# Attention scores of a causal kernel on one core: query and key parts as two float32r parts, two heads of a pair in the two row halves of the array

## The reference, cut to what matters

```
q, k = rotated (and in the first layer normalised) parts of x @ w_qkv
attn = einsum('bhqd,bhkd->bhqk', q, k) * scale        # D = 8 channels a head
attn = where(causal, attn, -inf); attn = softmax(attn)
out  = einsum('bhqk,bhkd->bhqd', attn, v)
```

```
scores = einsum('bhtd,bhsd->bhts', q, k) * mask        # decay in q and k
denom  = clip(abs(scores).sum(-1), 1, 50000)
ret    = einsum('bhts,bhsv->bthv', scores / denom, v)
```

## Time and profile before

| what | value |
|---|---|
| median of 3 runs | 2440.61 us (2437.79 to 2441.31) |
| the profiled execution, first to last instruction (span) | 2438.4 us |
| PE, DVE, ACT, POOL busy | 81%, 70%, 56%, 17% of the span |
| attention stages (first maximum to last output) | about 68 to 549, 1106 to 1588 and 1836 to 2320 us |
| stage of the retention heads | about 677 to 889 us |
| mean granted TensorE clock | 0.908 of full speed |

### The profile page before, as it was taken

How to read it: one execution, slowest core, us unless ns; L and a number is a source line. 1 busy time by engine, 2 the same in 40 slices (tenths; PEclk the granted TensorE clock), 3 DMA queues, 4 the chain that set the end, 5 groups by cost and what they waited for, 6 DMA issues and landing times. The chain is left out here.

```text
span 2438.4 us, 38777 instructions
## 1 busy us (share of the span) xinstructions
PE 1983.5 (81%) x13002; PEld 869.3 (36%) x13002; DVE 1703.7 (70%) x4395; ACT 1355.0 (56%) x1947; POOL 419.0 (17%) x670
## 2 busy tenths in 40 slices
PE   5689999994879974777799999957555899999939
PEld 3122333223534442553223333237331223332228
DVE  6688788847567767567788888632695887888433
ACT  4246666676379965334356666732543466666812
POOL 4000021020055521310001110133000010210133
PEclk9799999996989985988899999978867999999969
DMA  7600120001111100016101010014027001100024
GB/s 199 162 1 15 27 41 1 1 1 62 52 46 48 47 16 1 1 31 188 24 1 41 9 33 1 1 45 174 23 55 188 1 3 39 41 1 1 2 93 166
DMA packets 63781, 114.82 MB, mean 47 GB/s; under 512 B 12588, under 2 KB 45486, under 8 KB 62836
## 3 DMA queue, kind: packets, MB, share of 16 engines
q1 hardware_dynamic: 55668, 98.72, 14.9%
q0 software_dynamic: 5088, 11.24, 1.6%
q10 hardware_dynamic: 2860, 2.77, 0.3%
HBM read 64.78 MB, written 31.56 MB: 40 GB/s over the span
## 5 line engine op out<-in xcount | busy, mean ns | idle before, releaser
L1087 ACT ACTIVATE probs<-score 128x1024 f32<-128x1024 f32 x960 | 825.7, 897 | 542.2 <-PE score L1151 539.2
L1209 DVE TENSOR_REDUCE max_part<-stat 128x1 f32<-128x512 f32 x1152 | 721.9, 683 | 113.7 <-PE stat L1101 112.2
L1164 PE MATMUL pv<-probs,v_ones 128*9 128x512 f32 (+3 forms) x3840 | 443.7, 534 | 0.7 <-ACT out_turned L1078 0.5
L1206 DVE CUSTOM_DVE_ANT_0 masked_scores<-stat,mask_row 128x128 f32<-128x128 f32 (+3 forms) x768 | 343.2, 487 | 125.7 <-PE stat L1101 124.1
L1056 POOL TENSOR_SCALAR_AFFINE_SELECT probs<-probs 128x256 f32<-128x256 f32 x384 | 154.7, 408 | 1272.5 <-ACT probs L1087 1269.1
L1101 PE MATMUL stat<-first_group_k,first_group_q 128*128 128x512 bf16 (+2 forms) x960 | 301.1, 368 | 68.2 <-DVE max_part L1209 35.7
L1101 PE MATMUL stat<-group_k,group_q 128*128 128x512 bf16 (+2 forms) x960 | 288.5, 349 | 15.1 <-DVE max_part L1209 9.1
L1151 PE MATMUL score<-first_group_q,first_group_k 128*128 128x512 bf16 x960 | 262.8, 357 | 30.1 <-DMA first_group_q<-row_max_turned 29.0
L1151 PE MATMUL score<-group_q,group_k 128*128 128x512 bf16 x960 | 254.3, 350 | 5.8 <-DMA group_q<-row_max_turned 3.5
L1101 PEld LDWEIGHTS stat<-first_group_k,first_group_q 128*128 128x128 bf16 x960 | 93.9, 99 | 250.3 <-DVE max_part L1209 123.6
L1859 ACT ACTIVATE abs_act_ps<-abs_act_ps 128x1024 f32<-128x1024 f32 (+3 forms) x176 | 167.6, 952 | 27.8 <-PE abs_act_ps L1812 27.8
(11 more groups left out here) (369 smaller groups left out, 2318.3 us busy)
## 6 DMA issues: line engine op xcount, KB each, us to landing
tile_wv<-expert_wv SPq DMA_DIRECT2D x38, 512.0 KB
q_parts<-early_parts_t SPq DMA_DIRECT2D x20, 384.0 KB, 3.3
group_k<-k_parts SPq DMA_DIRECT2D x18, 384.0 KB
group_q<-q_parts SPq DMA_DIRECT2D x18, 384.0 KB
q_parts<-parts_t SPq DMA_DIRECT2D x17, 384.0 KB, 4.6
head_q<-q_parts SPq DMA_DIRECT2D x48, 96.0 KB
head_k<-k_parts SPq DMA_DIRECT2D x48, 96.0 KB
first_group_k<-k_parts SPq DMA_DIRECT2D x9, 384.0 KB
```

The lines of the kernel that those rows point to most:

```text
L1087: nc.scalar.activation(probs[:, n % PSLOTS, :, 0:width], sc[hp][:, :, 0:width], ACT.Exp, scale=scale).then_inc(expd.sem, 1)
L1164: last = nc.tensor.matmul(acc[32 * h:32 * h + D + 1, f:BANK], v9[:, kt, g * HG + h, :], probs[:, (2 * t + h // 2) % PSLOTS, h % 2, 0:BANK ...
L1206: nc.vector.tensor_tensor_reduce(masked[:, at % 2, 0:width], ring[n % RBANKS][:, 0:width], w["mask_row"][:, BANK - width:BANK], 1.0, NEG, ...
L1209: nc.vector.reduce_max(into, ring[n % RBANKS][:], AX.X).then_inc(stat_used.sem, 1)
```

## The change

Queries and keys are cut into two parts instead of three, each held as float32 and rounded to what the engine takes as float32r (`rounded` is a bitcast to that type). 2 x 2 x 8 = 32 rows carry a head. Rows are laid out in two halves of 64: head 0 and head 2 of a group in partitions 0 to 63 (32 product rows, 2 shift rows, constants), head 1 and head 3 in 64 to 127, and each score or maximum matmul names its half with `tile_position`. Row tensors have half as many columns (`PAIRS` = 2 instead of 4 heads) of twice the width. A group's rows come in four transfers of 16 partitions for keys and four for queries. The matmul that subtracts a part is float32r too. The retention heads keep one matmul over 128 rows, of which 96 are now zero. The constants of the padding come through an HBM tensor that the load stage fills.

```diff
-PARTS = 3
+PARTS = 2
 KROWS = PARTS * PARTS * D
+HROWS = 64
+PAIRS = HG // 2
...
+def rounded(ap):
+    return ap.bitcast(F32R)
...
+def head_rows(h):
+    return slice(HROWS * (h % 2), HROWS * (h % 2) + HROWS)
...
-    rows = k_dram.rearrange("(g h d) a t -> g (d a) h t", h=HG, d=D)
-    for a in parts:
-        eng.dma_start(tile[a * PARTS * D:(a + 1) * PARTS * D, :, cols], rows[g][:, :, cols]).then_inc(sig.sem, 16)
+    rows = k_dram.rearrange("(g p i d) a t -> g i (d a) p t", p=PAIRS, i=2, d=D)
+    for i in range(2):
+        for a in range(PARTS):
+            at = HROWS * i + a * PARTS * D
+            eng.dma_start(tile[at:at + PARTS * D, :, cols], rows[g, i][:, :, cols]).then_inc(sig.sem, 16)
...
                 for n in range(NQ):
                     turn(n)
-                    if n > 0:
-                        take_out(n - 1, 1)
                     if n + 2 < NQ:
                         project(n + 2)
                     take_out(n, 0)
-                take_out(NQ - 1, 1)
...
-        uq, uk = ([first_rows[n], k.sb(f"group_{what}", [P, HG, T], BF16, ctx)] for n, what in enumerate("qk"))
+        uq, uk = ([first_rows[n], k.sb(f"group_{what}", [P, PAIRS, T], F32, ctx)] for n, what in enumerate("qk"))
...
-                    last = nc.tensor.matmul(out[:, 0:width], uq[b][:, h, at:at + P], uk[b][:, h, c * BANK:c * BANK + width],
-                                            start=True, stop=True)
+                    rows = head_rows(h)
+                    last = nc.tensor.matmul(out[:, 0:width], rounded(uq[b][rows, h // 2, at:at + P]), rounded(uk[b][rows, h // 2, c * BANK:c * BANK + width]),
+                                            start=True, stop=True, tile_position=(rows.start, 0))
...
-                        last = nc.tensor.matmul(sc[hp][:, i, 0:BANK - f], uk[b][:, h, kt * P:(kt + 1) * P], uq[b][:, h, j * BANK + f:(j + 1) * BANK],
-                                                start=True, stop=True)
+                        rows = head_rows(2 * hp + i)
+                        last = nc.tensor.matmul(sc[hp][:, i, 0:BANK - f], rounded(uk[b][rows, hp, kt * P:(kt + 1) * P]),
+                                                rounded(uq[b][rows, hp, j * BANK + f:(j + 1) * BANK]), start=True, stop=True, tile_position=(rows.start, 0))
...
-        qm, km = (k.sb(f"head_{n}", [P, 2, T], BF16, ctx) for n in "qk")
+        qm, km = (k.sb(f"head_{n}", [P, 2, T], F32, ctx) for n in "qk")
...
-                ins = nc.tensor.matmul(a_ps[slot][:, b:min(b + BANK, width)], qm[:, par, i * P:(i + 1) * P],
-                                       km[:, par, at + b:at + min(b + BANK, width)], start=True, stop=True)
+                ins = nc.tensor.matmul(a_ps[slot][:, b:min(b + BANK, width)], rounded(qm[:, par, i * P:(i + 1) * P]),
+                                       rounded(km[:, par, at + b:at + min(b + BANK, width)]), start=True, stop=True)
```

More of the change, by code:

```diff
@@ L13 @@
 BF16 = mybir.dt.bfloat16
+F32R = mybir.dt.float32r
 I32 = mybir.dt.int32
@@ L115, in pad_rows @@
     for n, tile in enumerate((q_tile, k_tile)):
-        eng.dma_start(tile[KROWS:P].rearrange("r h t -> r (h t)"), w["pad"][n].partition_broadcast(P - KROWS)).then_inc(sig.sem, 16)
+        for i in range(2):
+            rows = tile[HROWS * i + KROWS:HROWS * i + HROWS].rearrange("r p t -> r (p t)")
+            eng.dma_start(rows, w["pad"][n].partition_broadcast(HROWS - KROWS)).then_inc(sig.sem, 16)
 def parts_stored(k):
@@ L1449, in chunk_stage, with _ @@
         with nc.Block() as block:
+            if not inner:
+                @block.sync
+                def _(sp):
+                    wait_parts(sp, parts_stored(k))
             @block.gpsimd
@@ L1870, in _ @@
                 for par in range(2):
-                    nc.vector.memset(qm[PADDED, par, :], 0.0).then_inc(q_padded.sem, 1)
+                    for rows in PADDED:
+                        nc.vector.memset(qm[rows, par, :], 0.0).then_inc(q_padded.sem, 1)
                 dve.wait_ge(cleared.sem, cleared.at(1))
@@ L2564, in shape_constants @@
         "c_qdecay": tiles(np.exp(gamma * (pos - T // 2)) / np.sqrt(decay_sum)),
-        "c_pad": np.repeat(np.array([[0], [0xBF80BF80]], dtype=np.uint32), HG * T // 2, axis=1).view(np.float32),
+        "c_pad": np.repeat(np.array([[0.0], [-1.0]], dtype=np.float32), PAIRS * T, axis=1),
         "c_kdecay": tiles(np.exp(gamma * (T // 2 - pos))),
```

143 lines of the change are left out of this document (72 added, 71 removed).

## The result

The changed kernel takes 2511.2 us (median of 4 runs, 2505.4 to 2518.0) against 2440.8 us before: a ratio of 1.029, interval 1.027 to 1.031. It is slower by 70 us; the forecast was 72 us faster, and 2511 lies outside the range of 2290 to 2460.

The account below looks back on a forecast made before the run. PE was taken as the bound by 0.2 us a step, DVE close behind. Attention 72 + qkv 6 - retention 2 = 76 us, less some 4, gives 72 faster: 2366, or 2368 us as run; range 2290 to 2460.

Parts of the forecast that it names:

- float32r on the engine: Score, maximum and retention matmuls: a float32r pass takes 0.22 us for 512 columns, like bf16, so almost no cost.
- Third part and transfers: Qkv stages lose the third part's casts, 6 us saved over four; transfers at stage starts 0, between -15 and +20.
- The halves: Attention stages: paired matmuls in two row halves take 0.24 us instead of 0.44, saving 72 us over three stages.
- my even stretch: First attention stage from 122 to 510 us, some 137 steps, where 22 us of gain was forecast.
- That only just covers full blocks: Around `pv`: DVE's three banks, 1.9 us of work, just cover 1.8 us from last maximum to next result.
- I take 0.22: Time in us of one float32r matmul of 512 columns, chosen between 0.22 and 0.44.
- the rival of 0.44 us a pass: Float32r streams like a float32 record: 2600 us, without overlap some 700 more; 20% together with a slower clock.
- The rule against the change: Skill's rule for weight loads: float32 weights don't get bf16's fast load; if true for float32r without overlap, pairs gain nothing.
- the upper end (+16): Retention heads: some 300 short matmuls of 128 columns cost twice as much, 16 us, mostly inside PE's slack; +2 taken.
- The clock: Rival in attention stages: PE relieved to 75% might fall to 1.2 GHz in places, step 3.7 us; 20% with slower float32r.
- The pair gains nothing: Rival for score and maximum matmuls: halves don't overlap or weight loads bind; 2432 to 2445 us, centre 2436; 22%.
- The slower side: Whole kernel: chance 0.22 that the change makes it slower, against 0.70 faster and 0.08 the same.

Follow-up runs that it names:

- The order experiments: One maximum's matmul of each step moved right behind `pv`: changed kernel 2426.7 us, kernel before 2390.0, two bf16 parts in halves 2274.6, three bf16 parts in halves 2312.0.

## Why the prediction was wrong, point by point

The path from before to after, measured: 2440.7, third part away with its bytes and the new layout of the rows 2383.8 (-57), halves 2337.1 (-47), twice the bytes 2393.3 (+56), float32r on the engine 2511.2 (+118).

- *Third part and transfers* were put at -6 and 0. Together they measured -57 + 56 = -1: the bytes did hardly change (114.8 to 113.9 MB), and PE's wait for the shift rows is 10.0 us after 10.6. Right to 5 us in the sum. What I didn't see is how much each would be worth alone, above all at the start of a stage: 12 us for the third part and 8 to 9 back for the bytes.
- *The halves* were put at 72 us and gave 47. The spacing was right to the hundredth of a microsecond (0.23 us from pair to pair, forecast 0.24); the size was off by a third. Behind the fourth copies they gave 55 us; ahead of them, where part of my even stretch lies, they took 7 back. The step that failed is "That only just covers full blocks": the 1.8 us from the last maximum to the next result was added up in rows of bf16 and for a score pair of 0.24 us, and was compared with 1.9 us of banks as if it fit. The order experiments show that it didn't, not even before the change, where moving one matmul gave 49 us.
- *float32r on the engine* was put at 0 in the attention stages and +2 in the heads, and cost some 118 us. This is the step on which the prediction failed: the passes of float32r were priced and its loads were not. Behind the fourth copy its 19 to 25 us a stage ate the 17 to 19 that the halves give in bf16, so that the stretch kept its 304.6 us in two stages; ahead of the copy it took 15 to 17 us a stage more. "I take 0.22" was nearly right for a stream (0.46 us a pair with full rows, 0.23 in halves), and the rival of 0.44 us a pass was wrong. The rule against the change, which I named and weighed lightly, is the one that the rows point to: the load of a float32r weight is the slow one, 186 to 189 ns here where a bf16 one has 97 and a float32 one 203. The Trainium skill (TensorE: Matmul & The Clock Gate, Weight-path perf modes) states it for float32; these rows carry it over to float32r. I asked only whether the two loads of a pair follow each other. They overlap; but a load after a wait, or after `pv`, is bare, and the step above has two of those.
- *The retention heads* grew by 19 us, of them 12 on the engine. The case that I had as the upper end (+16) came: the short matmuls did cost twice as much (111 against 56 ns, 14 us by the estimate above), and the slack that was to take it shrank from 40.7 to 15.2 us and the heads grew all the same. The other 7 us go with the bytes, which I had not counted here.
- *The clock* as I had it (a relieved PE falls to 1.2 GHz) didn't happen in the even part, which stays at 1.00 but for 3 us in the second stage and 14 in the third. It happened at the stages' starts, at a busy PE. Its price, by the estimate above some 12 us a stage, is spread over the terms: it would be why the halves lose at the starts, and since the lower level lasts 64 to 74 us with float32r and 40 to 52 with bf16 at twice the bytes, a part of the 118 may be the clock's too. How large, stays open.
- *The rivals.* "The pair gains nothing" came nearest in mechanism, with 22%; but its ground was not what happened, for the halves do overlap and do gain; it was priced at 2436 because the loads were counted once a pair, and not at the waits and in the heads. The slower side held 22% in all, and no case gave 2500.

## What to carry to other kernels

When an operand's type changes, price the weight load at every place where the engine has just waited, and not only under a full stream: that is where the results lie for which others wait. Before relieving the engine that looks busiest, add up the loop from the last result before its longest instruction to the first one behind it, against the buffers that cover it; a change in the order of one instruction is a cheap test of it. Cut a stage where its character changes before calling its loss even: here one stretch was unchanged in two of three stages, and the start had lost 14 to 16 us in each. And a change of two parts is best measured as two: here one part gave 47 us and the other took 118, and 56 more for its bytes.

## What the hardware showed beyond expectation

- With matmuls on 64 rows the granted clock stood at its lower level with PE busy 9.51 to 9.98 of 10 us; the same matmuls on 128 rows, busy 9.00 and 9.57, had 1.00 at that time. The lower level lasted 64 to 74 us ahead of a stage's fourth copy against 17 to 20, in bf16 32 to 40 against 0 to 3. Two full-row matmuls a step shortened it in the float32r kernel and lengthened it in the bf16 one.
- A float32r matmul of 512 columns is one record. In the stream of full rows a pair takes 0.46 us against 0.43 to 0.44 in bf16, and the first pair after `pv` 0.58 against 0.44. Short ones of 128 columns, each with its own weights, come every 111 ns against 56.
- Two 64-row matmuls with their loads run together at 0.23 us a pair in float32r (461.37 to 461.60) and in bf16 (460.13 to 460.36), where bf16 on full rows takes 0.44 a pair.
- An engine busy for 95% of a stretch (369.5 of 388 us) was not its bound: moving one matmul gave 2% of the kernel.
